# An early-fusion block on one core: the 22 unread products of a constant matrix ahead of the first group are taken out

## The reference

```python
h = tok(x, W, b, cls_token, pos_enc)            # patches @ W.T + b, class token ahead, + pos_enc
h = jnp.concatenate([h, txt], axis=1)           # (64, 114, 256)
h = h + attn(_layernorm(h), ...)                # W_in, causal conv of 4 taps, silu, scan over time, W_out
h = h + ffn(_layernorm(h), ...)                 # shared expert for all rows, top-1 of 8 experts for 512 rows
```

## Time and profile before

| | us |
|---|---|
| median of 3 runs | 1710.02 (1707.89 to 1710.78) |
| the profiled execution | 1707.03 |
| its span, first to last instruction | 1704.8 |
| busy: POOL / DVE / PE / ACT | 1562.6 (92%) / 1539.9 (90%) / 1485.8 (87%) / 1322.1 (78%) |
| mean granted clock of TensorE | 0.948 |

### The profile page before, as it was taken

The page is one execution under the profiler, slowest core; times in us unless marked ns, Lnnn a source line. Parts: engine busy times, 40 slices in busy tenths (PEclk is TensorE's granted clock), DMA queues, the critical chain, the costliest instruction groups (busy, mean ns, idle before and its releaser), DMA issues.

```text
span 1704.8 us, 27981 instructions
## 1 busy us (share of the span) xinstructions
PE 1485.8 (87%) x9868; PEld 1062.9 (62%) x9868; DVE 1539.9 (90%) x1360; ACT 1322.1 (78%) x3071; POOL 1562.6 (92%) x782
## 2 busy tenths in 40 slices
PE   7778898898998988988989889899898898987688
PEld 7555666666666666666666666666666666654355
DVE  2599999999999999999999999999999999998944
ACT  2577888888888888888888888888888888886644
POOL 0699999999999999999999999999999999999914
PEclk9898999999999999999999999999999999997799
DMA  5667665555666555556665555566655565656110
GB/s 142 141 135 183 166 139 124 125 128 132 147 131 148 136 123 125 131 131 145 133 148 134 125 123 132 133 144 133 148 134 123 124 132 133 139 125 140 40 35 16
DMA packets 194430, 218.47 MB, mean 128 GB/s; under 512 B 94011, under 2 KB 184773, under 8 KB 193778
## 3 DMA queue, kind: packets, MB, share of 16 engines
q1 hardware_dynamic: 193522, 215.51, 55.4%
q0 software_dynamic: 576, 1.17, 0.3%
q10 hardware_dynamic: 192, 0.01, 0.0%
HBM read 169.92 MB, written 47.09 MB: 127 GB/s over the span
## 4 chain that ended last, share of the span: by engine, by line
DVE 27%; POOL 25%; PE 16%; ACT 15%; issue 10%; DMA 5%; SPq 1%; DVEq 0%; ACTq 0%; POOLq 0%
POOL xr L1757 16%; DVE psum L1375 13%; ACT psum L1046 7%; DVE xr L1384 7%; DVE xr L1375 5%; POOL xr L1765 5%; PE psum L624 4%; POOL u L1778 3%; DMA u<-u_scratch 3%; PE psum L725 2%; ACT L1077 2%; PE psum L796 2%; ACT soft L1094 2%; PE psum L797 2%; ACT soft L1098 1%
## 5 line engine op out<-in xcount | busy, mean ns | idle before, releaser
L1757 POOL TENSOR_TENSOR xr<-u,bbc 128x912 f32<-128x912 f32 x512 | 1075.6, 2132 | 13.6 <-DMA u<-u_scratch 13.6
L1046 ACT ACTIVATE psum<-delta,a_neg 128x228 f32<-128x228 f32 x2048 | 804.9, 441 | 209.1 <-DVE xr L1384 178.8
L1375 DVE TENSOR_TENSOR_SCAN psum<-psum,xr 128x912 f32<-128x912 f32 x320 | 655.1, 2047 | 14.3 <-POOL xr L1757 8.4
L1765 POOL TENSOR_TENSOR xr<-xr,cbc 128x912 f32<-128x912 f32 x192 | 408.3, 2126 | 32.5 <-DVE xr L1375 32.3
L1375 DVE TENSOR_TENSOR_SCAN xr<-psum,xr 128x912 f32<-128x912 f32 x192 | 393.1, 2047 | 19.1 <-ACT psum L1046 19.1
L1384 DVE TENSOR_TENSOR xr<-psum,cbc 128x912 f32<-128x912 f32 x320 | 352.3, 1101 | 4.8
L725 PE MATMUL psum<-xr,fold 128*32 128x228 f32 x4096 | 297.4, 388 | 27.5 <-DVE xr L1384 14.7
L624 PE MATMUL psum<-xh,win 128*128 128x228 f32 x1024 | 220.3, 364 | 30.9 <-ACT xs L1077 24.9
L624 PEld LDWEIGHTS psum<-xh,win 128*128 128x128 f32 x1024 | 190.8, 191 | 57.4 <-ACT xs L1077 35.0
L675 PE MATMUL psum<-xi,conv_d 128*128 128x228 f32 x1024 | 211.4, 358 | 0.0
L675 PEld LDWEIGHTS psum<-xi,conv_d 128*128 128x128 f32 x1024 | 190.9, 189 | 16.4 <-issue 11.7
(11 more groups left out here) (207 smaller groups left out, 1550.1 us busy)
## 6 DMA issues: line engine op xcount, KB each, us to landing
delta<-delta_scratch SPq DMA_DIRECT2D x256, 228.0 KB, 6.6
u<-u_scratch SPq DMA_DIRECT2D x256, 228.0 KB, 4.3
bbc<-bc_scratch SPq DMA_DIRECT2D x128, 114.0 KB, 2.5
u_scratch<-u SPq DMA_DIRECT2D x64, 228.0 KB, 3.6
cbc<-bc_scratch SPq DMA_DIRECT2D x128, 114.0 KB, 2.7
delta_scratch<-delta SPq DMA_DIRECT2D x64, 226.0 KB, 5.6
out<-ob SPq DMA_DIRECT2D x32, 228.0 KB
h_scratch<-h SPq DMA_DIRECT2D x31, 228.0 KB
```

Of the source, the lines that this page charges most:

```text
L1046: ins = nc.scalar.activation(slot(k)[:, j * TOK:(j + 1) * TOK], delta4[:, c // 2, j, c % 2], ACT.Exp, scale=a_neg[:, c, j, n:n + 1])
L1375: nc.vector.tensor_tensor_scan(x if k in on_pool(i) else slot(k), slot(k), x, 0.0, ALU.mult, ALU.add).then_inc(scan_done, 1)
L1757: nc.gpsimd.tensor_tensor(xr[:, k % XRING], u4[:, c // 2, :, c % 2], bbc[:, p, n].unsqueeze(1).to_broadcast([P, J, TOK]), ALU.mult).then_i ...
L1765: nc.gpsimd.tensor_tensor(xr[:, k % XRING], xr[:, k % XRING], cbc[:, p, k % NI].unsqueeze(1).to_broadcast([P, J, TOK]), ALU.mult).then_inc ...
```

## The change

All three calls of `idle_turns` in `first()` go, and the helper with them: 22 products (44 MATMUL and 44 LDWEIGHTS records) on PE. No wait, no DMA and no other instruction is changed, added or moved.

```diff
-                    def idle_turns(n):
-
-                        for _ in range(n):
-                            pe.matmul(psum[:, YB, 0:P], mean_w[:], mean_w[:], start=True, stop=True)
-
                     def first():
 
                         pe.wait_ge(const_pool, CONST_POOL)
-                        idle_turns(12)
                         pe.wait_ge(token_in, TOKEN_IN)
                         tokens(0, 1)
                         pe.wait_ge(const_dve, DVE_TOKENS)
                         center(0)
-                        idle_turns(4)
                         var(0)
-                        idle_turns(6)
                         pe.wait_ge(conv_in, CONV_IN)
                         proj_x(0, 0, 0)
                         proj_x(0, 0, 1)
```

## The result

The changed kernel takes 1715.64 us in the median of 7 runs (1712.68 to 1716.32), the kernel before 1710.01 (1707.89 to 1710.78, 7 runs): the ratio is 1.003 with a 95% interval of 1.0019 to 1.0042, so it is slower by 3.2 to 7.2 us. The forecast was 1716.5, in a range of 1712 to 1720.

The account below looks back on a forecast made before the run. It took PE's serial chain at the front to decide, with POOL, DVE and PE busy later; -0.1 + 2.6 + 1.5 + 0.8 + 1.7 = 6.5 us on 1710.0 gave 1716.5 us, range 1712.0 to 1720.0.

Parts of the forecast that it names:

- Item 1: Ahead of group 0's tokens: the 12 products hide behind the token loads, so removing them gains only 0.1 us.
- 2. tokens: Group 0's 24 token records (line 639) run wholly at 1.2 GHz, 5.39 us for 2.80: a loss of 2.6 us.
- 3. centering: The 8 centering records of 228 columns run at 1.2 GHz from their start: a loss of 1.5 us.
- 4. variance: The variance runs at 1.2 GHz, 1.89 us for 1.05: a loss of 0.8 us, bounds 0 and 0.85.
- Item 5: The projection begins cold after PE's idle waits, 5.04 us for 3.32: a loss of 1.7 us.
- Passing through in full: From the front to the end: the DMA pieces move along whole, so all 6.5 us reach the total time.
- Rival A: In group 0's tokens: they raise the clock themselves, losing 1.65 us less 0.1, giving 1711.6 or 1713.3 us; chance 0.11.
- Rival C: From 66.81 to 80.5 us: PE runs warm after the shift, regaining 4.3 us; chance 0.06, with whatever else.

Follow-up runs that it names:

- second profile: The changed kernel, all 22 products gone, run and profiled once more: 1714.55 us against 1708.81 for the kernel before, ratio 1.0035.
- 8 columns: Kernel before with its unread products streaming 8 columns in place of 128, and 9, 2 and 3 of them: median 1717.82 us, ratio 1.0063.
- 38 products: Kernel before with 38 unread products in place of 12 ahead of the token wait: 1715.72 us against 1708.81, ratio 1.0043.
- both additions: Kernel before with 17 first products started at 1.1 us and 30 more in the wait for group 2's patches: 1703.27 us against 1708.81, ratio 0.9974.
- 28 late products: Kernel before plus 28 unread products while PE waits for the patches of group 2: median 1703.58 us against 1708.12, ratio 0.9988.

## Why the prediction was right

The path was right, and each of its five terms was within 0.25 us of the profile. By the two profiles:

| step | forecast | measured |
|---|---|---|
| 1. start of the tokens | -0.1 | -0.34 (7.79 for 8.13) |
| 2. tokens | +2.6 | +2.57 (5.37 for 2.80) |
| 3. centering | +1.5 | +1.60 (3.39 for 1.79) |
| 4. variance | +0.8 | +0.85 (1.90 for 1.05) |
| 5. projection | +1.7 | +1.94 (5.26 for 3.32) |
| front | +6.5 | +6.62 |

Item 1 was mis-sized. It was read off the landing of the loads in one execution (DVE at 7.90), and the smaller of two values was taken. In the profile of after the loads landed at 7.72 and PE began 0.07 later. But they land anywhere between 6.70 and 8.07, and at their mean, 7.3, the 12 cost 0.7 to 0.8 us of waiting, not 0.1. That the front of the profiles came out at 6.6 for 6.5 owes something to luck, since in both executions the loads landed late. Item 5 is 0.2 to 0.4 larger because the rise came 3.9 us into the projection (4.1 in the second profile), not 3.4 as in the row of before. Its price in microseconds lies between 1.6 (8 columns: 4.90) and 2.1 (5.40) in the five profiles whose projection began cold (before's 3.32 against 4.90 to 5.40).

*Passing through in full* was argued in the forecast and is shown by the 38 products: 6.49 in, 6.51 at POOL, 6.9 in the medians. One reading behind the argument was wrong: DMA is not silent from 22 us up to delta. In before its share is 0.60 and 0.86 in the two stretches from 32 to 34 us, when B is read back (line 511). That traffic hangs on PE too (line 699), so it moves along and nothing came of it.

*Rival A* (the tokens raise the clock themselves) is wrong in every one of the four executions that began with them or with 8 columns ahead of them: 5.37 us each time. That is where the Trainium skill's page "TensorE: Matmul & The Clock Gate" (section "The HAM clock gate"), by which the warm-up is a matter of time and not of the number of products, leads astray for this kernel; the runs decide against it. The half of A on the projection (it falls back in the waits) was right, and the kernels without the 6 show it.

*Rival C* did not happen: the tokens of group 2 took 5.39 us after the change as before. Its price, up to 4.3 us, was about right: the kernel with both additions, with a granted clock of 1.00 from 66 to 75 us, has line 711 some 4.0 us earlier beyond the tokens' own start.

The medians give 5.6 and 5.7 for the front's 6.6. The intervals reach from 3.2 to 8.0, so the missing microsecond is not established. The landing of the loads can account for most of it: items 2 to 5 lose 7.0 us, and at the mean landing the tokens start 0.7 to 0.8 earlier, which gives 6.2. That is an estimate from twelve single profiles; no run tests it.

## What to carry to other kernels

Products that nobody reads are not idle work if they stand ahead of a serial stretch of small products on PE: ask of each block on the chain at which level of the clock it runs, and what PE did ahead of it. Each call should be weighed by itself: here 12 were worth about 4 us, 6 about 1.7, and 4 nothing beside the others. What such products cost is read over several executions: where they outlast the wait that they fill, they delay the chain. The loss in such a front is the full difference only because nothing behind it has slack; a plain delay of the same size is a cheap way to test that. The places to look for more are the long waits on a DMA ahead of a cold block on the chain.

## What was not expected of the hardware

- PE can be drawn as busy without a gap for 9 us (3.80 to 13.03, products of 8 columns and then the tokens) and stay at 1.2 GHz. Its busy share alone does not tell the clock.
- The rise that came as the centering ended in one execution (8 columns) was gone again before the projection, with one variance and a few thin products between; the variance alone had the use of it. A clock that has risen is not a clock that stays up for the next block.
- The same 24 records of line 902, begun at 3.79 each time, took 4.51, 4.62 (with the 28 late products) and 4.79 us in three kernels: the rise comes at another point of the work from one execution to the next. The Trainium skill says so too, on the page and in the section named above ("run-variable"), and the traces agree: 0.28 us between the first and the last of these.
- In a trace that starts below the full clock, the clock column reads 1.00 until the first recorded change. The time per record (221 ns and 125 ns for the same product) is what tells the two levels apart there.
